# Causal attention between two expert layers on one Trainium2 core: six reads of q on ScalarE's queue, three in each of two steps, become two in each of three steps

## The chip, the cores and the metric

The kernel runs on one core of a Trainium2 chip. The metric is the device time of one execution in microseconds; less is better. The core's engines are TensorE (PE in the profile, its weight loads PEld), VectorE (DVE), ScalarE (ACT), GpSimd (POOL) and SyncE (SP), each with an instruction stream of its own that is worked off in order. They wait for each other on semaphores. SP, ACT and POOL also issue DMA transfers.

## The reference, cut to what matters

A macaron block over 32 sequences of 256 tokens with 128 channels: half an expert layer, causal self-attention, half an expert layer, each with a layer norm ahead and a residual around it. The change lies in the attention.

```python
x = L0_attn_batch                                    # 32 x 256 x 128
x = x + 0.5 * _L0_ffn_ref(_layernorm(x, axis=-1), ...)
x = x + _L0_attn_ref(_layernorm(x, axis=-1), ...)
x = x + 0.5 * _L0_ffn_ref(_layernorm(x, axis=-1), ...)

# inside _L0_attn_ref: 16 heads of 8 channels
qkv = sn_dense(batch, W_qkv, u_qkv, sigma_qkv)
q, k, v = jnp.split(qkv, 3, axis=-1)                 # then split into heads
att = jnp.einsum('bhqd,bhkd->bhqk', q, k) * scale
att = jnp.where(causal[None, None] == 0, big_neg, att)
att = jax.nn.softmax(att, axis=-1)
x = jnp.einsum('bhqk,bhkd->bhqd', att, v)
x = sn_dense(x, W_proj, u_proj, sigma_proj)
```

## The kernel before

The attention works through 32 sequences, one a **turn**. A turn has 12 **steps** (`u` from 0 to 11, `NP = 12`). Each engine has a function `turn(b, k, has)`, written out by hand: it walks through the steps and issues at each what belongs there, for several sequences at once. `has(o)` says whether sequence `b + o` exists. The function `run` emits four turns ahead of the first sequence and the first four, then a hardware loop of seven rounds with four turns each, then the last turns. The order on an engine is thus fixed, and the semaphores alone decide when things start.

What a turn does for the sequences:

- For sequence `b`, each step `u` computes scores by key into the PSUM tile `at_pm` (two buffers, PE L1161 and L1165). ScalarE takes their exponential into `at_pt` (L1080), GpSimd masks that (L1038), and PE multiplies it by `v` some steps later (L1182). PE may write the scores of a step only when ScalarE has taken the exponential of two steps before: `wait(pe, exped, b * NP + (u - 1))`.
- For sequence `b + 2` (and `b + 1`), PE computes scores by query (`at_pp`, L1143 to L1150) from which VectorE takes each query's maximum (L1296). The first of these for a new sequence stands in step 5 and waits for the reads of `q` and `k` (`qk_in`).
- For sequence `b + 3`: transposition of the normalised rows (L1194, copy by ScalarE L1083), projection to `q` and `k` (L1201, L1202), splitting into three bf16 parts (L1091, L1308, L1104, L1049), and the round through DRAM that brings them into the layout of the heads. SyncE writes the parts to `at_qkd` (L1005) and reads `k` back into `kb` with six transfers (L1012). ScalarE reads `q` back into `qs` with six transfers (L1128). These reads wait for the write to have landed (`part_out`).
- For sequence `b + 1`: the negated maxima in bf16 parts are transposed (PE L1242), copied by ScalarE (L1117) into `at_mt`, and at the end of step 8 moved into six rows of `qs` by a transfer of ScalarE's queue (L1119). The first scores by key of the next turn wait for it (`m_in`).
- For sequence `b - 2`: statistics (DVE L1272 to L1276), the power of the variance on GpSimd (L1043), the second normalisation (DVE L1280), its transposition (PE L1198).

The six reads of `q` are two halves (`r` = 0, 1) of 48 rows. Each half is cut into 24, 16 and 8 rows. Before the change ScalarE issues the three reads of half 0 behind the exponential of step 9 and the three of half 1 behind that of step 10. They are issued in program order by the same sequencer that starts the exponentials, so the exponential of step 10 stands behind three issues, and so does that of step 11.

Of the kernel before, what the change touches and what calls it, by code (L numbers as in the profile page):

```python
# [34 lines left out]
NQ = 4  # L35
# [6 lines left out]
def ds(start, n):  # L42
    return bass.ds(start, n)
# [851 lines left out]
def attention(nc, m, io, c, x_dram):  # L895
# [9 lines left out]
    with ctx:  # L905
# [52 lines left out]
        def wait(eng, s, n, most=None):  # L958

            if isinstance(n, int):  # L960
                n = n if most is None else min(n, most)
                if n <= 0:
                    return
            eng.wait_ge(s, n)

        def dma_count(b, slots, each=1):

            return lambda k: b * (16 * each // slots) + (16 * each - (k % slots) * (16 * each // slots))
# [10 lines left out]
        def run(eng, turn):  # L979
            emit = turns(turn)  # L980
            next(emit)
            with eng.Fori(1, B // NQ - 1) as i:
                for k in range(NQ):
                    turn(i * NQ + k, k, lambda o: True)
            next(emit)
# [84 lines left out]
        @blk.scalar  # L1070
        def _(act):
            a = nc.scalar
            act.wait_ge(zeroed, NZ)

            def turn(b, k, has):
                for u in range(NP):
                    if has(0):
                        wait(act, main_done, b * NP + (u + 1))
                        wait(act, pv_done, (b - 1) * PER_CG + (u // 3 + 1))
                        a.activation(pt[u % RING][:, :], pm[u % 2], ACT.Exp, scale=SCALE).then_inc(exped, 1)  # L1080
                    if u == 0 and has(3):
                        wait(act, xt_tr, (b + 4) * TPB)
                        a.activation(xt[(k + 1) % 2][:, :], mi[0][:, 0:S], ACT.Copy).then_inc(xt_out, 1)  # L1083
                    if u == 3 and has(-2):
                        wait(act, x2t_tr, (b - 1) * TPB)
                        a.activation(x2t[k % 2][:, :], mi[1][:, 0:S], ACT.Copy).then_inc(x2t_out, 1)
                    if u == 2 and has(3):
                        h = (k + 1) % 2
                        wait(act, qk_mm, b + 4)
                        wait(act, part_out[h], dma_count(b + 1, 2, 2)(h))  # L1090
                        a.activation(part[h][:, 0:6:5, :], mi[0].rearrange("p (a n) -> p a n", a=2), ACT.Copy).then_inc(a_done, 1)  # L1091
                    if u == 6 and has(-2):
                        wait(act, num_mm, b - 1)
                        a.activation(c.num[:, ds((b - 2) * TPB, TPB), :], mi[0][:, 0:TPB * E].rearrange("p (j e) -> p j e", e=E),
                                     ACT.Copy).then_inc(num_out, 1)
                    if u == 4 and has(-1):
                        wait(act, pv_done, b * PER_CG)
                        wait(act, otr, b - 2)
                        a.activation(ot[(k - 1) % 2][:, :, :].rearrange("p g q -> p (g q)"), po[(k - 1) % 2],
                                     ACT.Copy).then_inc(ot_out, 1)  # L1100
                    if u == 4 and has(3):
                        h = (k + 1) % 2
                        wait(act, r_done, b + 4)
                        a.activation(part[h][:, 1:5:3, :], rest[h][:, :].rearrange("p (a n) -> p a n", a=2), ACT.Copy).then_inc(b_done, 1)  # L1104
                    if u == 5 and has(3):
                        wait(act, v_mm, b + 4)
                        wait(act, pv_done, b * PER_CG)
                        a.activation(vp[(k + 3) % NQ][:, :, :, 0:HD].rearrange("p j h d -> p (j h) d"),
                                     mi[0][:, 0:TPB * D].rearrange("p (h d) -> p h d", d=HD), ACT.Copy).then_inc(v_out, 1)
                    if u == 7 and has(-1):  # L1110
                        wait(act, ont_tr, b)
                        a.activation(ont[(k - 1) % 2][:, :], mi[1][:, 0:S], ACT.Copy).then_inc(ont_out, 1)
                    if u == 8 and has(1):
                        q = (k + 1) % NQ
                        wait(act, mt_tr, b + 2)
                        wait(act, m_in[(q - 2) % NQ], dma_count(b - 1, NQ)(q - 2))
                        a.activation(mt[q % 2][:, :], mi[0].bitcast(BF16)[0:3 * H, 0:S], ACT.Copy).then_inc(mt_out, 1)  # L1117
                        wait(act, mt_out, b + 2)
                        act.dma_start(qs[q][ROWS:ROWS + 6, :, :], mt[q % 2][:, :].unsqueeze(1)).then_inc(m_in[q], 16)  # L1119
                    if u in (9, 10) and has(3):  # L1120
                        n, q, h, r = b + 3, (k + 3) % NQ, (k + 1) % 2, u - 9
                        if r == 0:
                            wait(act, main_done, (n - NQ + 1) * NP)
                            wait(act, part_out[h], dma_count(n, 2, 2)(h))
                        src = qkd[h].rearrange("(a g) n -> a g n", g=HP)
                        for row, size in ((0, 24), (24, 16), (40, 8)):
                            to = 48 * r + row
                            act.dma_start(qs[q][to:to + size, :, :], src[48 * r:48 * r + size, :, :]).then_inc(qk_in[q], 16)  # L1128
            run(act, turn)

        @blk.tensor
# [260 lines left out]
```

## Time and profile before

| | us |
|---|---|
| median of 3 runs | 1376.95 |
| lowest and highest of the 3 | 1375.21, 1379.9 |
| the profiled execution, its own time | 1371.16 |
| the profiled execution's span | 1369.4 |
| PE busy in the span | 1025.8 (75%) |
| ACT busy in the span | 596.7 (44%) |

The span is the time from the first to the last instruction of the program. The profile is of one execution. Its page gives for each engine the busy time, then the span in 40 slices, and further views of the trace answer who waited for whom and list instructions in order of time. A row of the timeline has the start in us from the span's start, the length in us, the engine, the line, the operation, the tiles written and read, the shape, the number of merged instructions and, in brackets, how long the engine had been idle before it and what ended that. ACTq and SPq are the sequencers' issues of transfers; they do not count as busy time of the engine.

### The profile page before, as it was taken

Reading aid. Unit: us, or ns where it says so; the run is one execution under the profiler, and the core shown is the slowest. Engines: PE = TensorE matmul, PEld = TensorE weight load, DVE = VectorE, ACT = ScalarE, POOL = GpSimd, SP = SyncE. Lnnn points to the kernel's source line nnn. Section 1 sums busy time; section 2 is a strip of 40 time slices with the busy share of each in tenths; the row PEclk is TensorE's granted clock in tenths of the full one; section 3 lists DMA queues with packets and bytes.
Section 4 is the critical chain, followed back from the end, with each engine's and each line's share of the span. In section 5 each row is a group of like instructions: output and inputs, shape, how many; then the busy total and the mean of one; then the engine's idle time right before and its main releaser. Section 6 shows DMA issues by size and latency. Waiting matters only on the chain. (4 is left out here: it accounts for less than half of the span.)

```text
span 1369.4 us, 29600 instructions
## 1 busy us (share of the span) xinstructions
PE 1025.8 (75%) x8390; PEld 783.3 (57%) x8390; DVE 735.9 (54%) x2124; ACT 596.7 (44%) x1498; POOL 644.3 (47%) x1022
## 2 busy tenths in 40 slices
PE   1586735787777479999999999999866636777776
PEld 1475515677677246566656566556545515767776
DVE  6476792222222367777777777777626782222212
ACT  4023303334334146666666666666533303434434
POOL 3350005666665135565555555555530006666664
PEclk9657956999989599999999999999977857999989
DMA  4350001111111354445454554444200001111110
GB/s 139 86 159 6 0 0 38 42 43 40 40 40 30 70 102 92 95 96 94 100 99 97 99 99 98 103 99 91 57 17 0 0 0 43 41 43 42 38 42 25
DMA packets 115112, 83.72 MB, mean 61 GB/s; under 512 B 13307, under 2 KB 105523, under 8 KB 115030
## 3 DMA queue, kind: packets, MB, share of 16 engines
q1 hardware_dynamic: 90262, 46.85, 15.8%
q10 hardware_dynamic: 15552, 17.71, 6.1%
q0 software_dynamic: 9216, 18.15, 5.2%
q8 instruction: 42, 0.69, 0.2%
q14 instruction: 40, 0.33, 0.1%
HBM read 52.23 MB, written 30.67 MB: 61 GB/s over the span
## 5 line engine op out<-in xcount | busy, mean ns | idle before, releaser
L1296 DVE TENSOR_REDUCE at_mx<-at_pp 128x2 f32<-128x512 f32 (+1 forms) x384 | 260.4, 686 | 102.6 <-PE at_pp L1150 60.6
L1038 POOL TENSOR_SCALAR_AFFINE_SELECT at_pt<-at_pt 128x256 f32<-128x256 f32 (+1 forms) x384 | 183.3, 488 | 216.6 <-ACT at_pt L1080 215.9
L1080 ACT ACTIVATE at_pt<-at_pm 128x512 f32<-128x512 f32 x384 | 224.4, 597 | 123.4 <-PE at_pm L1161 78.3
L807 ACT ACTIVATE e_ht<-e_ps_h,b1t 128x128 f32<-128x128 f32 x576 | 163.7, 375 | 213.9 <-remote 93.3
L775 POOL DMA_INDIRECT e_x<-rows,gidx x144 | 140.4, 975 | 241.7 <-issue 143.0
L835 PE MATMUL e_ps_h<-e_xnt,e_w1own 128*128 128x128 f32 x1152 | 178.1, 303 | 89.6 <-ACT e_xnt L801 58.8
L835 PEld LDWEIGHTS e_ps_h<-e_xnt,e_w1own 128*128 128x128 f32 x1152 | 162.1, 217 | 98.2 <-ACT e_xnt L801 63.1
L881 DVE SCALAR_TENSOR_TENSOR e_y<-e_ps_y,e_x 128x256 f32<-128x256 f32 x72 | 30.6, 425 | 304.9 <-PE e_ps_y L845 149.1
L845 PE MATMUL e_ps_y<-w,e_ht 128*128 x1152 | 178.3, 299 | 13.2 <-issue 13.0
L845 PEld LDWEIGHTS e_ps_y<-w,e_ht 128*128 128x128 f32 x1152 | 155.9, 208 | 15.9 <-issue 13.1
L1161 PE MATMUL at_pm<-qs,kb 128*128 128x256 bf16 x512 | 98.7, 274 | 20.0 <-ACT at_pt L1080 19.9
L1182 PE MATMUL at_po<-at_pt,vp 128*32 128x256 f32 (+1 forms) x2048 | 111.7, 336 | 1.0 <-POOL at_pt L1038 1.0
L784 POOL DMA_INDIRECT out_dram<-e_y,sidx x72 | 76.6, 1063 | 65.4 <-DVE e_y L881 48.7
L784 POOL DMA_INDIRECT x<-e_y,sidx x72 | 76.3, 1060 | 65.9 <-DVE e_y L881 49.4
L1148 PE MATMUL at_pp<-kb,qs 96*128 96x512 bf16 x256 | 100.2, 392 | 1.7 <-DVE at_mx L1296 0.8
L801 ACT ACTIVATE e_xnt<-e_ps_x 128x256 f32<-128x256 f32 x72 | 28.2, 392 | 139.0 <-PE e_ps_x L828 124.3
L1182 PEld LDWEIGHTS at_po<-at_pt,vp 128*32 128x32 f32 x2048 | 54.0, 110 | 51.0 <-issue 15.4
L1161 PEld LDWEIGHTS at_pm<-qs,kb 128*128 128x128 bf16 x512 | 47.3, 98 | 61.8 <-DMA qs<-at_mt 17.1
L656 DVE SCALAR_TENSOR_TENSOR r_beats<-r_ps_b,r_amax,tie 128x256 f32<-128x256 f32 x128 | 56.9, 482 | 33.6 <-PE r_ps_b L597 33.6
L1150 PE MATMUL at_pp<-mask,identb 128*128 128x256 bf16 x256 | 71.1, 278 | 0.0
L875 DVE COPY e_w1own<-w 128x512 f32 x144 | 61.5, 429 | 16.6 <-remote 12.6
L597 PE MATMUL r_ps_b<-r_batcht 128*128 128x256 f32 x256 | 68.2, 390 | 0.0
(257 smaller groups left out, 1737.2 us busy)
## 6 DMA issues: line engine op xcount, KB each, us to landing
at_qkd<-at_part SPq DMA_DIRECT2D x64, 192.0 KB, 2.9
kb<-at_qkd SPq DMA_DIRECT2D x64, 96.0 KB
qs<-at_qkd ACTq DMA_DIRECT2D x64, 96.0 KB
rows<-ts_x ACTq DMA_DIRECT2D x16, 264.0 KB, 2.9
rows<-at_x SPq DMA_DIRECT2D x32, 132.0 KB, 3.9
ts_x<-in_x_dram SPq DMA_DIRECT2D x16, 256.0 KB, 3.5
at_xa<-x SPq DMA_DIRECT2D x32, 128.0 KB, 3.4
qs<-at_qkd ACTq DMA_DIRECT2D x64, 64.0 KB
```

The source lines that it names most:

```text
L775: pool.indirect_dma_start(x_row[s][:, j % 2, :], None, rows, bass.IndirectOffsetOnAxis(ap=c.gidx[:, j:j + 1], axis=0)).then_inc(x_in[s], 16)
L784: pool.indirect_dma_start(y_dram, bass.IndirectOffsetOnAxis(ap=c.sidx[:, j:j + 1], axis=0), y_row[s][:, j % 2, :], None, bounds_check=T - ...
L807: last = a.activation(hid_t[j % NB][:, f, :], ps_h[j % NB][:, f, :], ACT.Gelu, bias=c.b1t[:, ds(e, 1), f])
L835: last = te.matmul(ps_h[j % NB][:, f, :], w1_own[j % NB][:, f * P:(f + 1) * P], xn_t[(j // 2) % NX][:, j % 2, :], start=True, stop=True, s ...
L845: last = te.matmul(out, hid_t[j % NB][:, f, :], c.w2[:, ds(e, 1), f, :].rearrange("p a d -> p (a d)"), start=False, stop=(f == FC - 1))
L1038: g.affine_select(out=tile, in_=tile, compare_op=ALU.is_ge, fill=0.0, base=0, pattern=[[0, n], [1, P]], channel_multiplier=-1).then_inc(ma ...
L1080: a.activation(pt[u % RING][:, :], pm[u % 2], ACT.Exp, scale=SCALE).then_inc(exped, 1)
L1148: te.matmul(out, qs[s][0:ROWS, v - 4, P:S], kb[s][0:ROWS, v - 4, :, :].rearrange("p r q -> p (r q)"), start=True, stop=False, skip_group_c ...
L1150: te.matmul(out.rearrange("p (r q) -> p r q", r=2)[:, :, P:S], c.identb[:, :], c.mask[:, 0:2, :], start=False, stop=True, skip_group_check ...
L1161: last = te.matmul(out[:, i * S:(i + 1) * S], kb[s][:, g + 2 * w + i, r, 0:P], qs[s][:, g + 2 * w + i, :], start=True, stop=True)
L1182: last = te.matmul(out[32 * j:32 * j + 32, (half + 1) * S - cols:(half + 1) * S], values[:, w // 2, at:at + 32], src[:, i * cols:(i + 1) * ...
L1296: v.tensor_reduce(out, src, axis=AX.X, op=ALU.max).then_inc(maxed, 1)
```

## The change

The condition `u in (9, 10)` becomes `u >= 9`. Steps 9, 10 and 11 each issue one size (24, 16, 8 rows) for both halves. The two waits (`main_done`, `part_out`) stay at the first of the six. Nothing is added or removed: the same six transfers with the same bytes on the same queue and the same semaphore `qk_in`.

```diff
-                    if u in (9, 10) and has(3):
-                        n, q, h, r = b + 3, (k + 3) % NQ, (k + 1) % 2, u - 9
-                        if r == 0:
+                    if u >= 9 and has(3):
+                        n, q, h = b + 3, (k + 3) % NQ, (k + 1) % 2
+                        if u == 9:
                             wait(act, main_done, (n - NQ + 1) * NP)
                             wait(act, part_out[h], dma_count(n, 2, 2)(h))
                         src = qkd[h].rearrange("(a g) n -> a g n", g=HP)
-                        for row, size in ((0, 24), (24, 16), (40, 8)):
+                        row, size = ((0, 24), (24, 16), (40, 8))[u - 9]
+                        for r in range(2):
                             to = 48 * r + row
                             act.dma_start(qs[q][to:to + size, :, :], src[48 * r:48 * r + size, :, :]).then_inc(qk_in[q], 16)
```

In the loop's body, ScalarE's rows from the copy of the maxima in step 8 (L1117) to the second exponential of the next turn stand like this before the change. L1080 are the exponentials, L1119 is the transfer of the maxima, L1128 the reads of `q`, L1083 the copy of the transposed rows.

```order
L1117 ACTIVATE at_mt<-at_mi 48x256
L1119 DMA qs<-at_mt 6x8x256
L1080 ACTIVATE at_pt<-at_pm 128x512
L1128 DMA qs<-at_qkd 24x2048
L1128 DMA qs<-at_qkd 16x2048
L1128 DMA qs<-at_qkd 8x2048
L1080 ACTIVATE at_pt<-at_pm 128x512
L1128 DMA qs<-at_qkd 24x2048
L1128 DMA qs<-at_qkd 16x2048
L1128 DMA qs<-at_qkd 8x2048
L1080 ACTIVATE at_pt<-at_pm 128x512 x2
L1083 ACTIVATE at_xt<-at_mi 128x256
```

The last row but one is the exponential of step 11 and that of the next turn's step 0, with nothing between them. The same place on ScalarE with the change:

```order
L1117 ACTIVATE at_mt<-at_mi 48x256
L1119 DMA qs<-at_mt 6x8x256
L1080 ACTIVATE at_pt<-at_pm 128x512
L1129 DMA qs<-at_qkd 24x2048 x2
L1080 ACTIVATE at_pt<-at_pm 128x512
L1129 DMA qs<-at_qkd 16x2048 x2
L1080 ACTIVATE at_pt<-at_pm 128x512
L1129 DMA qs<-at_qkd 8x2048 x2
L1080 ACTIVATE at_pt<-at_pm 128x512
L1083 ACTIVATE at_xt<-at_mi 128x256
```

The exponential of step 10 now stands behind two issues, that of step 11 behind two more, and two have moved past it to stand ahead of the exponential of step 0. The instructions of the other engines keep their order.

## Rows read from the trace of the kernel before

**Rows 1.** The page: busy time in us and its share of the span.

```profile
PE 1025.8 (75%) x8390; PEld 783.3 (57%) x8390; DVE 735.9 (54%) x2124; ACT 596.7 (44%) x1498; POOL 644.3 (47%) x1022
```

**Rows 2.** Windows of the attention: length, then busy time of PE, PEld, DVE, ACT, POOL, clock, DMA share, GB/s.

```profile
700.00:800.00 100.00, 93.52 (x925) 60.12 (x922) 73.88 (x189) 63.15 (x129) 58.57 (x124) 1.00 0.52 99
```

**Rows 3.** Waits in total: us, times, longest.

```profile
PE at_pm L1161 <- ACT at_pt L1080: 19.9, 32, 2.4
```

**Rows 4.** Timeline of PE from step 11 to step 0 of two turns.

```profile
704.92 0.39 PE L1161 MATMUL at_pm<-qs,kb 128*128 128x256 bf16 x2 [0.61 <-ACT at_pt L1080]
...
720.34 0.27 PE L1150 MATMUL at_pp<-mask,identb 128*128 128x256 bf16 x1
721.24 0.38 PE L1161 MATMUL at_pm<-qs,kb 128*128 128x256 bf16 x2 [0.63 <-ACT at_pt L1080]
```

**Rows 5.** Timeline of ScalarE, from the transfer of step 8 to step 1 of the next turn.

```profile
717.97 0.75 ACTq L1119 DMA_DIRECT2D qs<-at_mt  x1
718.91 0.60 ACT L1080 ACTIVATE at_pt<-at_pm 128x512 f32<-128x512 f32 x1 [0.97 <-PE at_po L1182]
719.01 1.31 ACTq L1128 DMA_DIRECT2D qs<-at_qkd  x3
720.49 0.60 ACT L1080 ACTIVATE at_pt<-at_pm 128x512 f32<-128x512 f32 x1 [0.98 <-PE at_pm L1165]
720.51 1.30 ACTq L1128 DMA_DIRECT2D qs<-at_qkd  x3
721.98 1.08 ACT L1080 ACTIVATE at_pt<-at_pm 128x512 f32<-128x512 f32 x2 [0.89 <-PE at_pm L1161]
722.95 0.39 ACT L1083 ACTIVATE at_xt<-at_mi 128x256 f32<-128x256 f32 x1
723.35 1.15 ACT L1080 ACTIVATE at_pt<-at_pm 128x512 f32<-128x512 f32 x2
```

**Rows 6.** All issues of L1128: duration in ns, min/median/max.

```profile
L1128 ACTq DMA_DIRECT2D qs<-at_qkd x192: 295/374/1017, 463.6 to 967.3; - x192
```

**Rows 7.** Timeline: the three issues behind step 9, each alone.

```profile
719.01 0.31 ACTq L1128 DMA_DIRECT2D qs<-at_qkd  x1
719.35 0.37 ACTq L1128 DMA_DIRECT2D qs<-at_qkd  x1
719.75 0.58 ACTq L1128 DMA_DIRECT2D qs<-at_qkd  x1
```

**Rows 8.** Timeline from step 1 to step 4: GpSimd, VectorE, PE.

```profile
724.49 1.01 POOL L1043 TENSOR_TENSOR at_x<-at_vare,at_powers 128x4 f32<-128x4 f32 x1
725.53 0.60 DVE L1280 TENSOR_SCALAR at_xn<-at_x 128x128 f32<-128x128 f32 x2 [1.10 <-POOL at_x L1043]
726.19 0.44 PE L1198 MATMUL at_mi<-ident,at_xn 128*128 128x128 f32 x2
727.39 0.71 PE L1214 MATMUL at_mi<-wv,at_xt 128*128 128x128 f32 x4 [0.21 <-DVE at_rest L1308]
```

**Rows 9.** Timeline of the first turn: the transfer of the maxima, and the weight load that waits for it.

```profile
487.23 0.89 ACTq L1119 DMA_DIRECT2D qs<-at_mt  x1
489.84 0.11 PEld L1161 LDWEIGHTS at_pm<-qs,kb 128*128 128x128 bf16 x2 [0.55 <-DMA qs<-at_mt]
```

**Rows 10.** SyncE's reads of k and their first use on PE, in a middle turn and in a late one.

```profile
718.88 4.37 SPq L1012 DMA_DIRECT2D kb<-at_qkd  x6
727.93 0.38 PE L1143 MATMUL at_pp<-kb,qs 96*128 96x256 bf16 x2
964.98 4.34 SPq L1012 DMA_DIRECT2D kb<-at_qkd  x6
973.58 0.39 PE L1143 MATMUL at_pp<-kb,qs 96*128 96x256 bf16 x2 [0.33 <-DMA kb<-at_qkd]
```

**Rows 11.** Windows around those reads, columns as in Rows 2.

```profile
721.00:727.00 6.00, 5.70 (x60) 3.62 (x60) 4.30 (x14) 4.13 (x9) 4.08 (x8) 1.00 0.93 170
727.00:731.00 4.00, 3.79 (x42) 2.72 (x41) 3.32 (x8) 3.10 (x7) 1.85 (x3) 1.00 0.01 2
```

## The prediction

> **What bounds the kernel now.** I read the page first, to see where TensorE is full. PE is the busiest engine, 1025.8 us [rows 1]. The windows then show how full PE is within the attention: 93.52 us busy in 100, at granted clock 1.00, VectorE 73.88, ScalarE 63.15 [rows 2]. So a turn of the attention has only 7% of idle time on PE, and a change can give back no more than what part of that it reaches. The length of a turn is read from PE's first scores of step 0 in two turns: 721.24 - 704.92 = 16.32 us [rows 4], of which 7% is 1.1 us.
>
> The list of waits names the largest piece: the scores by key of L1161 wait for ScalarE's exponentials 32 times, 19.9 us together, 0.62 us a turn [rows 3]. The timeline says which scores these are. They are those of step 0: PE ends L1150 at 720.34 + 0.27 = 720.61 and starts them at 721.24, idle 0.63 us, released by L1080, and the turn before the same with 0.61 us [rows 4]. They need the exponential of step 10, the one at 720.49, which ends at 721.09 [rows 5].
>
> Why is that exponential late? ScalarE sat idle 0.98 us before it. The bracket names PE's L1165, but what stands directly ahead of it in the program are three issues of reads, from 719.01 for 1.31 us, to 720.32. The exponential starts 0.17 us later. The same again: three issues from 720.51 for 1.30 us, to 721.81, and the exponential of step 11 at 721.98, 0.17 us later [rows 5]. Had PE set the time, the distance of 0.17 would not come out the same twice. In these steps ScalarE's sequencer, not its arithmetic and not its input, sets the pace.
>
> **The change, step by step.** All times are those of this turn [rows 5 to 7].
>
> *Step 9.* The issues cost 0.31, 0.37 and 0.58 us with gaps of 0.04 us. Two of them end at 719.72 instead of 720.32. The exponential of step 10 then starts at 719.72 + 0.17 = 719.89 and ends at 720.49, 0.60 us earlier. PE has its own work until 720.61. So the scores of step 0 can start at about 720.65, 0.59 earlier, if nothing else holds them.
>
> *Step 10.* The next two issues follow at 719.91. The third issue of a batch took 0.58 us where the median of all 192 is 0.374; I take 0.58 for the first of the two (it is the third in a row, and comes just where that one came) and 0.37 for the other, with 0.04 between: to 720.90. The exponential of step 11 starts at 721.07 instead of 721.98.
>
> *Step 11, where the two moved issues cost something.* From 721.09 two at 0.41, a little over the median, and 0.04 between them: to 721.95, and the exponential of step 0 at 722.12. Before, it stood right behind that of step 11: the two together end at 721.98 + 1.08 = 723.06, so it started at about 722.46. It comes 0.34 us earlier, not 0.59. Behind it are the copy L1083 (722.95 before, 722.61 now; its input from L1194 would be there 0.59 earlier) and the exponential of step 1 (723.35 before). They too come 0.34 us earlier, 0.41 if the last two issues take the median.
>
> *What is late next.* From the exponential of step 1 a chain leads to PE: the mask, the power at 724.49 behind it on GpSimd, the normalisation L1280 that waited 1.10 us for it, and the transposition L1198 at 726.19, right when L1280 ends at 726.13; L1214 waits 0.21 us on VectorE behind that [rows 8]. These come earlier by what the exponential of step 1 gains. So PE wins 0.59 us at step 0 and gives about 0.2 back at steps 2 to 4. What is left for the turn is the gain of ScalarE's row of issues, 0.34 to 0.41 us; I take 0.38.
>
> *What the change costs at nothing.* The bytes are the same. The DMA engines are 0.93 busy from 721 to 727 and idle from 727 on [rows 11]. SyncE's reads of k are issued from 718.88 to 723.25, ScalarE's last now until 721.95 instead of 721.81 [rows 5, 10]; so the last transfers to land are still those of SyncE's queue. Their first use is at 727.93 [rows 10], 0.9 us after the traffic stops. That is the cover of the moved reads; with a turn that reaches step 5 some 0.4 us earlier it shrinks to about 0.5.
>
> A rule of the Trainium skill speaks against any gain here. "DMA: Bandwidth & Descriptors", section "Issuing engines are not separate DMA queues", says that the time a sequencer needs to start a transfer is usually small beside the transfer. By it the position of six issues would be worth next to nothing, and the time would stay at 1377. The trace does not bear it out for this place, since 1.31 us of issue stand ahead of an exponential that PE waits for. The same section says that transfers of all queues share 16 DMA engines and interleave; with that the trace agrees, and by it the later reads neither gain nor lose.
>
> *The sum.* The exponentials run in 32 turns. Reads of q stand beside them in 29, those that have a sequence b + 3. I leave the first of these out, which fills the pipeline: 28 turns by 0.38 us = 10.6 us. The profiled execution took 1371.16 us, so it would take 1360.5. It lies 5.8 us below the median of the three runs shown, 1376.95, and I add that back: **1366.3 us**, 0.8% faster.
>
> **Bounds.** The unknown price is what an issue takes in its new place. The lowest of the 192 is 0.295, the third of a batch 0.58, the longest 1.017 us [rows 6, 7]. With 0.37 for all of the last four, PE's own floor of 0.59 us a turn is reached: 16.5 us, 1360.4. With the mean of the batches instead (1.30 us for three, 0.43 each with its gap), the row gains what was reckoned, 0.3 to 0.4 us. The break-even is worked out like this. From the exponential of step 10 at 719.89 to 722.46, where that of step 0 stood, are 2.57 us. Two starts (0.02 and 0.17 us each) and two gaps take 0.46, so four issues may take 2.11, 0.53 each.
>
> **The rivals.**
>
> *The whole wait goes (chance 0.08).* The last four issues take the median or less and the copy L1083 is held by PE alone. For it: the median. Against it: three issues in a row take 1.31 and 1.30, not 1.2. Gain 0.55 to 0.62 a turn, 1360.
>
> *A landing holds PE in place of the exponential (0.13).* There are two places. One is the transfer of the maxima, for which the same scores of step 0 wait. In the first turn, where no exponential hides it, PE's weight load came 489.84 - 487.23 = 2.61 us after its issue [rows 9]. In the turn above that is 717.97 + 2.61 = 720.58, just ahead of PE's own 720.61; it costs nothing, but 0.4 us more would eat most of the gain. The other is the first use of k and q in step 5. In a late turn PE waited for it, 973.58 - 964.98 = 8.60 us after SyncE's first read [rows 10]. In the turn above that is 718.88 + 8.60 = 727.48, where the forecast wants PE at 727.93 - 0.38 = 727.55. So the gain ends at 0.45 a turn, and if the reads land 0.4 later in most turns, it is gone: 1373 to 1377.
>
> *Slower (0.08).* The moved issues are as slow as the third of a batch, 0.58 each, because ScalarE and SyncE issue at once. Then: 719.91 + 1.20 = 721.11, exponential of step 11 at 721.28, two more until 722.50, exponential of step 0 at 722.67, 0.21 us later than before. The copy, the exponential of step 1 and the chain to L1198 follow: 28 by 0.21 = 5.9 us, 1383. It decides from 0.53 us an issue on. For it: SyncE issues until 723.25. Against it: the second batch took 1.30 for three while SyncE was issuing too.
>
> The likeliest case has 0.71, its own range is 1361 to 1371 (0.2 to 0.55 us a turn).
>
> **How the numbers follow.** A difference under 0.3%, 4.1 us, is about what a measurement of this kernel can't tell from none. The first rival and most of the likeliest case are faster by more: 0.08 + 0.70 = 0.78. The landing case and the rest are the same: 0.14. Slower 0.08. The range from 1359 to 1375 takes in both good cases and the better part of the landing case; above it lie the rest of that and the slower one.
>
> **What the profile of the changed kernel would show.** Pairs of issues instead of triples, 0.7 to 0.8 us behind step 9; the exponential of step 10 some 1.0 us behind that of step 9 instead of 1.58; PE's wait ahead of step 0 near zero, total far below 19.9; the exponential of step 0 no longer right behind that of step 11; a turn of 15.9 us instead of 16.3; a new wait of PE at L1198 of about 0.2 us. The prediction is wrong if pairs take over 1.1 us in steps 10 and 11, if PE's wait only changes its name to a transfer (the maxima at step 0, or kb and qs at L1143), or if the time goes while PE's wait stays.

## The result: 0.27% faster, a third of the forecast

The changed kernel takes 1374.68 us (median of 22 runs), the kernel before 1376.85 us (median of 22). The ratio is 0.9973, interval 0.9961 to 0.9985: 2.1 to 5.4 us are gained, 3.7 in the middle. (The two medians lie 2.2 us apart and the two means 3.6; gains in time are given by the ratio, here and below.) The forecast was 10.6 us.

The profiled execution of the changed kernel has a span of 1375.3 us at a mean granted clock of 0.865. Its page has these busy times.

```profile
PE 1039.5 (76%) x8359; PEld 790.3 (57%) x8390; DVE 737.2 (54%) x2124; ACT 595.6 (43%) x1498; POOL 646.4 (47%) x1022
```

In the view of waits, two lines answer to [rows 3] (engine, its line, what it waited for: us in total, times, the longest). Line numbers from the edit on are one higher than before.

```profile
PE at_pm L1162 <- ACT at_pt L1080: 4.1, 5, 2.1
PE at_mi L1199 <- DVE at_xn L1281: 16.8, 31, 3.4
```

Of the 32 waits of [rows 3], 19.9 us together, 5 with 4.1 us are left. The wait at the transposition L1199 is 16.8 us. In the kernel before that list had this line for it:

```profile
PE at_mi L1198 <- DVE at_xn L1280: 12.2, 15, 3.4
```

It comes twice as often after the change. By the timelines PE waits 0.21 us there in an ordinary turn, where it waited for nothing before, and 0.68 instead of 0.52 us in a turn at the loop's end. So the change did what it says, and a part came back where the forecast expected it.

ScalarE's timeline of one turn, to be read against [rows 5] (start in us, duration, what; q behind the engine's name means its queue issues a transfer; in brackets the idle time before and who ended it):

```profile
723.23 0.75 ACTq L1119 DMA_DIRECT2D qs<-at_mt  x1
724.17 0.60 ACT L1080 ACTIVATE at_pt<-at_pm 128x512 f32<-128x512 f32 x1 [0.97 <-PE at_pm L1162]
724.27 0.72 ACTq L1129 DMA_DIRECT2D qs<-at_qkd  x2
725.15 0.60 ACT L1080 ACTIVATE at_pt<-at_pm 128x512 f32<-128x512 f32 x1 [0.39 <-PE at_pm L1162]
725.17 1.17 ACTq L1129 DMA_DIRECT2D qs<-at_qkd  x2
726.50 0.60 ACT L1080 ACTIVATE at_pt<-at_pm 128x512 f32<-128x512 f32 x1 [0.75 <-PE at_pm L1162]
726.52 0.78 ACTq L1129 DMA_DIRECT2D qs<-at_qkd  x2
727.48 0.60 ACT L1080 ACTIVATE at_pt<-at_pm 128x512 f32<-128x512 f32 x1 [0.38 <-PE at_po L1183]
727.98 0.38 ACT L1083 ACTIVATE at_xt<-at_mi 128x256 f32<-128x256 f32 x1
728.24 1.09 ACT L1080 ACTIVATE at_pt<-at_pm 128x512 f32<-128x512 f32 x2
```

Three pairs, 0.72, 1.17 and 0.78 us. The exponential of step 10 stands 0.98 us behind that of step 9 (725.15 - 724.17). The pair behind it is the dear one. The single issues of the second and third pair:

```profile
725.17 0.54 ACTq L1129 DMA_DIRECT2D qs<-at_qkd  x1
725.74 0.60 ACTq L1129 DMA_DIRECT2D qs<-at_qkd  x1
726.52 0.43 ACTq L1129 DMA_DIRECT2D qs<-at_qkd  x1
726.98 0.32 ACTq L1129 DMA_DIRECT2D qs<-at_qkd  x1
```

PE, at the place of [rows 4]:

```profile
725.60 0.27 PE L1151 MATMUL at_pp<-mask,identb 128*128 128x256 bf16 x1
725.89 0.38 PE L1162 MATMUL at_pm<-qs,kb 128*128 128x256 bf16 x2
```

The scores of step 0 start 0.02 us behind the matmul ahead of them (725.60 + 0.27 = 725.87), where it was 0.63 us.

### The end of the loop

The attention's loop body holds four turns, k = 0 to 3. The fourth (k = 3) ends with the loop's branch, right behind step 11. The loop has six rounds, not seven as the section on the kernel before says: it is `Fori(1, B // NQ - 1)` with B = 32 and NQ = 4 and works through sequences 4 to 27; the first four sequences are written out ahead of it and the last four behind it. So it jumps back five times, and "the turn at the loop's end" is one of those five. I had read no such turn. Here is one in the kernel before:

```profile
750.64 0.75 ACTq L1119 DMA_DIRECT2D qs<-at_mt  x1
...
753.20 1.22 ACTq L1128 DMA_DIRECT2D qs<-at_qkd  x3
754.58 1.12 ACT L1080 ACTIVATE at_pt<-at_pm 128x512 f32<-128x512 f32 x2 [0.80 <-PE at_pm L1161]
```

and in the changed kernel:

```profile
755.16 0.75 ACTq L1119 DMA_DIRECT2D qs<-at_mt  x1
...
758.38 0.60 ACT L1080 ACTIVATE at_pt<-at_pm 128x512 f32<-128x512 f32 x1 [0.70 <-PE at_pm L1162]
758.39 0.86 ACTq L1129 DMA_DIRECT2D qs<-at_qkd  x2
759.78 0.60 ACT L1080 ACTIVATE at_pt<-at_pm 128x512 f32<-128x512 f32 x1 [0.81 <-PE at_po L1183]
...
771.93 0.74 ACTq L1119 DMA_DIRECT2D qs<-at_mt  x1
```

Before, the exponentials of steps 11 and 0 form one row of two. After, the last pair of issues ends at 758.39 + 0.86 = 759.25, and the exponential of step 0 starts 0.53 us behind it, where it was 0.18 in the ordinary turn (727.48 - 726.52 - 0.78). From the issue L1119 it stands 759.78 - 755.16 = 4.62 us off. PE feels it twice (in an ordinary turn it has no such wait at L1166, and 0.21 us at L1199):

```profile
760.43 0.40 PE L1166 MATMUL at_pm<-qs,kb 128*128 128x128 bf16 x4 [0.28 <-ACT at_pt L1080]
...
763.85 0.44 PE L1199 MATMUL at_mi<-ident,at_xn 128*128 128x128 f32 x2 [0.68 <-DVE at_xn L1281]
```

The last round ends with the same instructions, but there the loop doesn't jump back. In the changed kernel:

```profile
953.08 0.85 ACTq L1129 DMA_DIRECT2D qs<-at_qkd  x2
954.17 0.60 ACT L1080 ACTIVATE at_pt<-at_pm 128x512 f32<-128x512 f32 x1 [0.50 <-PE at_po L1183]
```

Here the exponential of step 0 starts 954.17 - 953.08 - 0.85 = 0.24 us behind the last issue, where it is 0.53 to 0.55 in all five turns with the jump.

### All turns together

The table is worked out from the timelines: a turn runs from one issue L1119 to the next, and each entry is a median over the turns of that kind in one trace: 15 ordinary ones, from the loop's second round on, and the five at the loop's end. "Stretch" is from the third of these issues to the last, 29 turns, and leaves the start-up out. The names are those of the experiments below.

| kernel | ordinary turn | turn at the loop's end | stretch | six issues of q, in order |
|---|---|---|---|---|
| before | 16.33 | 16.71 | 474.1 | .31 .37 .62 .39 .38 .41 |
| before, again (e6) | 16.32 | 16.71 | 473.3 | |
| changed | 16.01 | 16.77 | 468.7 | .31 .38 .53 .60 .50 .32 |
| changed, again (e5) | 16.02 | 16.77 | 468.7 | |
| sizes in the new order, three and three (e8) | 16.46 | 16.95 | 478.0 | .31 .38 .68 .45 .65 .32 |
| pairs, sizes in the old order (e1) | 15.84 | 16.53 | 465.4 | .31 .37 .47 .54 .32 .33 |
| the same, again (e11) | 15.70 | 16.52 | 465.7 | |
| last pair in the next turn (e4) | 15.71 | 16.08 | 459.0 | .30 .38 .53 .60, .28 .36 |
| the same, again (e12) | 15.71 | 16.09 | 459.1 | |
| changed, SyncE quiet meanwhile (e7) | 16.19 | 16.20 | 470.5 | .31 .38 .32 .44 .28 .32 |
| before, SyncE quiet meanwhile (e10) | 16.78 | 16.79 | 490.1 | .31 .37 .33 .30 .38 .33 |
| last two of the old order in the next turn (e9) | 16.29 | 16.47 | 475.2 | .30 .37 .46 .54, .32 .33 |
| changed, old order in the start-up (e2) | 16.00 | 16.76 | 469.1 | |
| changed, old order where k is 3 (e3) | 16.00 | 16.71 | 467.5 | |

The stretches can be read from one row each. These are the rows of the tile at_mt in the window from the third turn on (count, shortest, median and longest issue in ns, first and last start), of the kernel before, of the changed one, and of both again (e6, e5):

```profile
L1119 ACTq DMA_DIRECT2D qs<-at_mt x30: 741/748/782, 520.6 to 994.7; - x30
```

```profile
L1119 ACTq DMA_DIRECT2D qs<-at_mt x30: 740/748/781, 527.4 to 996.1; - x30
```

```profile
L1119 ACTq DMA_DIRECT2D qs<-at_mt x30: 740/748/782, 522.5 to 995.8; - x30
```

```profile
L1119 ACTq DMA_DIRECT2D qs<-at_mt x30: 741/748/782, 521.5 to 990.2; - x30
```

474.1 and 473.3 us before, 468.7 and 468.7 after: 5.0 us gained in the mean, 1.3 more than the middle of the timing and within its interval. So the gain is made where the forecast put it, and all but a little of what can be told apart lies there.

The start-up, the first two turns, shows where a single trace misleads. In the changed kernel they took 527.4 - 492.4 = 35.0 us, against 520.6 - 487.2 = 33.4 before. At that place TensorE's granted clock was 0.57 in this execution (columns as in [rows 2]):

```profile
498.00:502.00 4.00, 3.45 (x14) 2.38 (x15) 0.35 (x1) 2.45 (x6) 1.46 (x3) 0.57 0.87 118
```

I first took the 1.6 us for a cost of the new order. The experiments e2, e3 and e5 are against it.

### The profile page after: what moved, and what is told of

Same layout as the page of the kernel before. It is cut to its first block and busy times, and to the rows that moved or that the text cites. A ratio compares the mean times of both kernels' runs of the same rounds, so it can differ in the third digit from the quotient of the medians.

```text
span 1375.3 us, 29569 instructions
## 1 busy us (share of the span) xinstructions
PE 1039.5 (76%) x8359; PEld 790.3 (57%) x8390; DVE 737.2 (54%) x2124; ACT 595.6 (43%) x1498; POOL 646.4 (47%) x1022
## 5 line engine op out<-in xcount | busy, mean ns | idle before, releaser
L1080 ACT ACTIVATE at_pt<-at_pm 128x512 f32<-128x512 f32 x384 | 226.1, 599 | 116.7 <-PE at_pm L1162 75.1
L845 PE MATMUL e_ps_y<-w,e_ht 128*128 x1152 | 187.6, 304 | 33.0 <-issue 32.9
L881 DVE SCALAR_TENSOR_TENSOR e_y<-e_ps_y,e_x 128x256 f32<-128x256 f32 x72 | 30.6, 425 | 311.5 <-PE e_ps_y L845 187.0
L845 PEld LDWEIGHTS e_ps_y<-w,e_ht 128*128 128x128 f32 x1152 | 161.1, 211 | 42.6 <-issue 39.9
L1183 PEld LDWEIGHTS at_po<-at_pt,vp 128*32 128x32 f32 x2048 | 53.8, 110 | 50.8 <-issue 14.6
```

Of the source, the lines that this page charges most:

```text
L845: last = te.matmul(out, hid_t[j % NB][:, f, :], c.w2[:, ds(e, 1), f, :].rearrange("p a d -> p (a d)"), start=False, stop=(f == FC - 1))
L1183: last = te.matmul(out[32 * j:32 * j + 32, (half + 1) * S - cols:(half + 1) * S], values[:, w // 2, at:at + 32], src[:, i * cols:(i + 1) * ...
```

## The experiments

The kernels e1 to e4 ran on a chip on which every kernel was about 7% shorter (the kernel before took 1279.16 us there, its experts' stages were the shorter part), so their ratios and their turns are compared, not their times. In the diffs, `plan` lists for steps 9, 10 and 11 what is read: (half of the heads, first row, rows). Each is given against the changed kernel, but for e10.

### e1: pairs, in the order of sizes that the kernel had before

The diff is two edits: it spreads the issues over three steps, and it reads equal sizes of both halves together (24, 24, 16, 16, 8, 8 in place of 24, 16, 8, 24, 16, 8). This kernel makes the first alone.

```
-                        row, size = ((0, 24), (24, 16), (40, 8))[u - 9]
-                        for r in range(2):
+                        plan = (((0, 0, 24), (0, 24, 16)), ((0, 40, 8), (1, 0, 24)), ((1, 24, 16), (1, 40, 8)))
+                        for r, row, size in plan[u - 9]:
```

> Two issues a step as in the changed kernel, but in the order of sizes of the kernel before (24, 16 then 8, 24 then 16, 8). Theory 'place' (an issue is slow because of where it stands behind the first two, whatever its size): the pairs of steps 10 and 11 take as long as in the changed kernel, about 1.15 and 0.85 us, the exponential of step 0 starts 4.3 us after the transfer of step 8, the turn is 16.0 us. Rival 'size' (the two reads of 16 rows side by side are dear): the pair of step 10 falls to 0.8 to 0.9 us, the turn to 15.8 us, and the time to 3 us below the changed kernel. In both, the start-up turn is as short as before the change (14.7 us, no half clock), since the order in it is that of before: 2 us below the changed kernel from that alone.

Measured: 1267.79 against 1279.16 us, ratio 0.9898 (0.9871 to 0.9925). The placement alone is worth more than the whole diff. Its stretch is 943.2 - 477.8 = 465.4 us, its pairs are cheaper than those of the changed kernel (.47 and .54 in step 10, .32 and .33 in step 11). On the chip of e11 the same code gained less, 0.6%.

### e2: the order of before in the start-up

```
+                        plan = NEW if has(0) else OLD
```

NEW and OLD stand for the orders of the changed kernel and of the one before.

> The changed kernel, but the turns ahead of the first exponentials keep the order 24, 16, 8, 24, 16, 8. Theory 'start-up': the order alone makes the six issues 0.57 us longer in the last of these turns, TensorE idles 2.03 instead of 1.46 us and its clock is halved for some 4 us; with the old order the first turn is 14.7 instead of 16.6 us, and the time is 2 us below the changed kernel, about 4 us below the kernel before (ratio 0.997 to 0.996). Rival 'chance': the half clock was an accident of that profile; then the ratio stays at 0.9973 and the first turn shows no fixed relation to the order.

Measured: 1272.85 us, ratio 0.9946 (0.9928 to 0.9964). Its first two turns took 473.4 - 441.5 = 31.9 us:

```profile
L1119 ACTq DMA_DIRECT2D qs<-at_mt x3: 741/762/889, 441.5 to 473.4; - x3
```

That looked as if the start-up were the culprit, until the next run.

### e3: the order of before in the turns at the loop's end

```
+                        plan = OLD if k == 3 and has(0) else NEW
```

> The changed kernel, but every fourth turn (the last of a loop round) has three issues in two steps as before. Theory 'loop end': with issues in step 11 the branch of ScalarE stands behind them instead of under the exponential, and the gain of the other turns (0.33 us) is lost in this one; with the old arrangement that turn takes 16.7 us, as in both kernels, and the ratio stays within 0.001 of the changed kernel's. Rival: the loop end costs the same in both; then the last turn of a round loses its 0.33 us, seven times, and the time rises by 2.3 us over the changed kernel's.

Measured: 1274.0 us, ratio 0.9962 (0.9941 to 0.9984). The turn at the loop's end went from 16.77 to 718.17 - 701.45 = 16.72 us:

```profile
701.45 0.75 ACTq L1119 DMA_DIRECT2D qs<-at_mt  x1
...
718.17 0.74 ACTq L1119 DMA_DIRECT2D qs<-at_mt  x1
```

That is the length it has in the kernel before, 16.71. So the new order loses some 0.05 us in each of the five turns with the jump. The edit also reaches the turn ahead of the loop and the one that ends its last round, where nothing jumps back. These get longer with the old order, 16.57 instead of 16.44 and 16.62 instead of 16.25 us. And this kernel starts up in the new order, in 474.6 - 443.5 = 31.1 us, where e2 took 31.9 in the old one:

```profile
L1119 ACTq DMA_DIRECT2D qs<-at_mt x3: 741/762/892, 443.5 to 474.6; - x3
```

The theory of a dear start-up falls with it.

### e4: the last pair in the next turn

ScalarE reads the two pieces of 8 rows in step 2 of the next turn, behind that step's exponential, so nothing is issued in step 11 and nothing stands ahead of the loop's branch. The start-up keeps the order of before.

```
+                    if u == 2 and has(-1) and has(2):
+                        q, h = (k + 2) % NQ, k % 2
+                        src = qkd[h].rearrange("(a g) n -> a g n", g=HP)
+                        for r in range(2):
+                            to = 48 * r + 40
+                            act.dma_start(qs[q][to:to + 8, :, :], src[48 * r:48 * r + 8, :, :]).then_inc(qk_in[q], 16)
```

> Two issues in steps 9 and 10, none in step 11; the two reads of 8 rows are issued in step 2 of the next turn, behind its exponential, where ScalarE waits 0.4 us for PE. The turns ahead keep the old order. Theory 'ScalarE's row of issues is the bound': the exponential of step 0 stands right behind that of step 11, the copy L1083 is set by PE, the turn falls by another 0.2 to 0.3 us to about 15.75, also at the loop's end (16.7 to 16.2): 28 turns by 0.6 = 16 us below the kernel before, ratio 0.989. Rival 'another bound lies close behind' (the landing of q and k at step 5, the power on GpSimd): PE waits at L1144 or L1199 grow by as much, and the ratio stays above 0.994.

Measured: 1261.32 us, ratio 0.9859 (0.9831 to 0.9887). Both kinds of turn are 0.6 us shorter than before, 15.71 and 16.08. The stretch is 931.1 - 472.1 = 459.0 us:

```profile
L1125 ACTq DMA_DIRECT2D qs<-at_mt x30: 741/748/787, 472.1 to 931.1; - x30
```

### e5 and e6: both kernels again

The same code on another chip.

> The changed kernel itself, timed beside the kernel before on the chip of this set. From the turns of its profile (21 turns of 16.33 become 16.01 us, 7 turns at the end of a loop round go from 16.71 to 16.77) the sum is 21 x 0.32 - 7 x 0.06 = 6.3 us. Theory 'the turns are all': the ratio is about 0.995. Rival 'the start-up takes 1.9 us back each time': the first turn of the attention is again 16.6 us and the ratio is 0.997.

> The kernel before once more, for its profile: turns of 16.3 us and 16.7 at the end of a loop round, reads of q at 0.31, 0.37, 0.6, 0.39, 0.38, 0.41 us. Of interest are the first two turns of the attention (14.7 and 18.7 us in the first profile): theory 'chance' has them scatter by 1 us and more between executions of one kernel, with half-clock stretches of TensorE at other places; the theory of an order that costs has them at 33.4 us together again.

Measured: e5 1366.6 against 1370.07 us, ratio 0.9965 (0.9944 to 0.9985); e6, one run, 1369.42. The first two turns took 32.4 us in the changed kernel (489.1 to 521.5) and 32.0 in the one before (490.5 to 522.5).

Over all traces they take 30.6 to 36.0 us, in no relation to the order of the reads: e1 and e11 are the same kernel and stand at the two ends. The median of the ordinary turns repeats within 0.01 us between the two traces of before, of the changed kernel and of e4. In e1 and e11 it differs by 0.14, but there single turns lie between 15.6 and 16.4 us, and the means of the two agree, 15.88 and 15.86.

### e7: SyncE doesn't issue while ScalarE does

In the changed kernel SyncE now begins its reads of k only when the exponential of step 11 is done.

```
+                    if has(0):
+                        sp.sem_inc(passed, 1)
+                        wait(sp, exped, b * NP + NP)
```

> The changed kernel, but SyncE issues its six reads of k only after the exponential of step 11, so ScalarE's six issues run alone. The whole gets slower, since k arrives later (PE waits at step 5); of interest is the price of ScalarE's issues. Theory 'contention with SyncE': the third to the fifth fall from 0.5 to 0.6 us to 0.3 to 0.4 us, the exponential of step 11 starts 2.8 us after the transfer of step 8 instead of 3.27. Theory 'ScalarE's own queue': they stay at 0.5 and 0.6.

Measured (one run): 1366.0 us. ScalarE's pairs, at its own line numbers:

```profile
719.79 0.72 ACTq L1132 DMA_DIRECT2D qs<-at_qkd  x2
...
720.69 0.79 ACTq L1132 DMA_DIRECT2D qs<-at_qkd  x2
...
721.66 0.62 ACTq L1132 DMA_DIRECT2D qs<-at_qkd  x2
```

0.79 and 0.62 us where the changed kernel has 1.17 and 0.78. Everything else on ScalarE's queue is the same, so the surplus comes with SyncE's six reads. For reads of 8 rows at least, e12 says that it is their issuing and not their transfers: its two late reads are issued when SyncE has done issuing its reads of k but the DMA engines are still 0.95 busy, and they take .28 and .36 us, the price that 8 rows have alone. SyncE pays nothing for the company. Its six issues take 4.37 us in the kernel before [rows 10] and here, where ScalarE is silent:

```profile
722.26 4.37 SPq L1015 DMA_DIRECT2D kb<-at_qkd  x6
```

The second 16-row read takes 0.44 us even here, against 0.32 for the first. The time doesn't fall with it, since k now lands too late for step 5:

```profile
PE at_pp L1147 <- DMA kb<-at_qkd: 10.5, 22, 1.0
```

### e8: the order of sizes alone

Three and three, as before, in the order 24, 24, 16 and 16, 8, 8.

```
+                        plan = (((0, 0, 24), (1, 0, 24), (0, 24, 16)), ((1, 24, 16), (0, 40, 8), (1, 40, 8)), ())
```

> Three issues in two steps as before the change, but in the order of sizes of the changed kernel (24, 24, 16, then 16, 8, 8). Theory 'place': the third is slow (0.6 us) whatever it is, the others 0.37 to 0.41, turn 16.3 us, ratio 1.000. Rival 'two of 16 rows in a row are dear': the fourth takes 0.6 too, the exponential of step 11 comes 0.2 us later, the turn is 16.4 to 16.5 us, ratio 1.002 to 1.003.

Measured: 1375.36 against 1370.07 us, ratio 1.0032 (1.0012 to 1.0051). It is slower than the kernel before. Its batches:

```profile
719.40 1.44 ACTq L1129 DMA_DIRECT2D qs<-at_qkd  x3
...
721.02 1.50 ACTq L1129 DMA_DIRECT2D qs<-at_qkd  x3
```

1.44 and 1.50 us for the same six reads that took 1.31 and 1.30 [rows 5]. With e1 and e11 this takes the diff apart: the placement gains 8 us or more, and the order of sizes loses 4 to 5 (4.4 here).

### e9: the last two reads of the old order in the next turn

Built from e1 and e4: 24, 16 in step 9, 8, 24 in step 10, and the second half's 16 and 8 in step 2 of the next turn.

```
+                        for row, size in ((24, 16), (40, 8)):
+                            to = 48 + row
+                            act.dma_start(qs[q][to:to + size, :, :], src[48:48 + size, :, :]).then_inc(qk_in[q], 16)
```

> As the version with a late pair (two reads in steps 9 and 10, two in step 2 of the next turn), but with the sizes in the order of the kernel before: 24, 16, then 8, 24, and late 16, 8. Theory 'PE is the bound there, ScalarE's issues no longer are': cheaper issues change nothing, turn 15.7 us, ratio as with the late pair, 0.986 to 0.988 on whatever chip. Rival 'the row of issues is still the bound': the turn falls by the 0.1 us that the exponential of step 11 gains, to 15.6, 3 us more.

Measured: 1369.52 against 1372.36 us, ratio 0.9992 (0.9971 to 1.0014). No gain, where e4 gains over 1%. The list of waits says why:

```profile
PE at_pp L1150 <- DMA qs<-at_qkd: 10.7, 18, 1.2
```

The same line in e4's second run (e12):

```profile
PE at_pp L1150 <- DMA qs<-at_qkd: 2.5, 5, 1.3
```

In the median the last piece of q lands 9.82 us behind L1119 in e9, against 9.00 in e12, and PE waits for it 18 times. (The expectation named neither outcome: both its theories had the time at or below e4's.) A piece of 16 rows that late is too late, where one of 8 is just in time.

### e10: the kernel before, with SyncE quiet

e7's wait, put into the kernel before.

> The kernel before the change, but SyncE issues its six reads of k only after the exponential of step 11. Theory 'contention with SyncE': the third read of each batch falls from 0.6 to about 0.35 us, each batch of three from 1.3 to about 1.05, the exponential of step 10 starts 2.3 instead of 2.56 us after the transfer of step 8, that of step 11 at 3.5 instead of 4.0. Theory 'a third issue in a row is slow by itself': 0.6 stays.

Measured (one run): 1385.46 us. The batches of three:

```profile
728.08 1.07 ACTq L1131 DMA_DIRECT2D qs<-at_qkd  x3
...
729.33 1.06 ACTq L1131 DMA_DIRECT2D qs<-at_qkd  x3
```

1.07 and 1.06 against 1.31 and 1.30 [rows 5]: in the kernel before, too, each batch paid 0.24 us for SyncE's company. The late k costs more than that gives:

```profile
PE at_pp L1146 <- DMA kb<-at_qkd: 17.6, 28, 1.3
```

### e11 and e12: the two that gained, on one chip

The code of e1 and of e4 again, side by side.

> The kernel with pairs in the order of sizes of before, once more, beside the late pair and beside the kernel before on one chip. The theory that the change is two edits, a placement that gains and an order of sizes that loses, asks for the same turns as in its first run (15.84 us, 16.53 at a loop's end): 21 x 0.49 + 7 x 0.18 = 11.5 us below the kernel before, ratio 0.991 to 0.992. If the ratio is 0.995 or more, as that of the changed kernel, the order is not what took the gain.

> The kernel with the 8-row reads moved to step 2 of the next turn, once more, beside the others. With its turns of 15.71 and 16.08 us: 28 x 0.62 = 17.4 us below the kernel before, ratio 0.987. Rival: the landing of q and k holds PE at step 5, as it does for 0.3 us a turn when the late pair carries 16 and 8 rows; then 0.990 or more, with waits of PE at L1150.

Measured against 1377.67 us: e11 1368.93, ratio 0.9938 (0.9919 to 0.9957); e12 1363.93, ratio 0.9897 (0.9870 to 0.9924). Their stretches:

```profile
L1119 ACTq DMA_DIRECT2D qs<-at_mt x30: 740/748/782, 522.6 to 988.3; - x30
```

```profile
L1125 ACTq DMA_DIRECT2D qs<-at_mt x30: 740/748/787, 527.0 to 986.1; - x30
```

465.7 and 459.1 us. Against the mean of the kernel before, 473.7, that is 8.0 and 14.6 us less, and the ratios say 8.5 and 14.2. For the other two kernels the stretch agrees as well: changed -5.0 (ratios: -3.7 and -4.8), order alone +4.3 (ratio: +4.4). The attention's stretch thus accounts for the timings to within 1.5 us on these chips. Both kernels stay some 3 us below what was expected, 11.5 and 17.4 us, which were again a median turn's gain times a count of turns. On the chip of e1 to e4 the ratios say more than the stretches, 13.0 us for e1 and 18.0 for e4 against 8.3 and 14.7; the kernel before has no trace from that chip, so where the other 3 to 5 us come from stays open. In e12 ScalarE's row from step 10 to step 0 is free of issues at its end:

```profile
720.65 1.17 ACTq L1135 DMA_DIRECT2D qs<-at_qkd  x2
721.99 1.09 ACT L1080 ACTIVATE at_pt<-at_pm 128x512 f32<-128x512 f32 x2 [0.76 <-PE at_pm L1168]
```

The dear pair is still there, 1.17 us, but the exponentials of steps 11 and 0 stand together again. The pair of 8-row reads takes 0.68 us in its new place, where a gap is:

```profile
724.06 0.68 ACTq L1092 DMA_DIRECT2D qs<-at_qkd  x2
```

e12 is the best version: 1% less than the kernel before, and four times the gain of the change.

## Why the prediction was too high

The mechanism, the place and the sign were right; the gain was 3.7 us where 10.6 were forecast. Two terms of the sum were wrong: the gain of a turn, "I take 0.38", and above all the count of turns that have it, "28 turns". That 1374.7 us still lies in the range of 1359 to 1375 is luck. Its upper part was there for a late landing, which didn't happen.

**Step 9, right.** The exponential of step 10 was to come 0.60 us earlier. By the medians it starts 1.92 us behind L1119 instead of 2.56, 0.64 earlier. PE's wait at step 0 was to go to near zero: 19.9 us [rows 3] became 4.1.

**Step 10, mis-sized.** The second pair was put at 0.99 us (0.58 + 0.04 + 0.37) and took 1.17 (0.54 and 0.60). I took the price of an issue by its rank in a batch. The trace of before holds no second 16-row read behind a first one while SyncE issues. e1 has the old neighbours and pays .47 and .54 for this pair, 0.12 us less than the changed kernel, so the new order of sizes accounts for most of the 0.18 us by which the pair was underrated. What lies above the quiet price of .32 and .44 goes with SyncE's issuing (e7).

**Step 11, right in sum.** The third pair was put at 0.86 and took 0.78 in the turn shown (0.82 by the medians of its issues). With the surplus of step 10 the exponential of step 0 comes 0.17 us earlier, 4.32 instead of 4.49, and not 0.34.

**What is late next, right in kind.** The turn depended on the exponential of step 1 and the chain to the transposition; I had moved that exponential by the same amount as the one of step 0. It gained more, 5.08 instead of 5.41, 0.33 us, since with its input ready it starts close behind the copy: 728.24, which is 0.26 us after the copy's start, where it was 0.40 [rows 5]. This gave back what the dear pair took. The ordinary turn is 0.32 us shorter in the median, 16.01 instead of 16.33, close to the 0.38 that I took. The median hides a pattern, though: the first turn of a round gains 0.15 us, the second and the third 0.35. The wait at L1198, now L1199, grew by 4.6 us in all and is 0.21 us in an ordinary turn; 0.2 was forecast.

**The count of turns, the step that failed.** I multiplied one turn's gain by 28, as if all 28 turns were the one that I had read. The timelines, with the mean of two traces of each kernel, say what the 28 did:

| turns | forecast | measured |
|---|---|---|
| five at which the loop jumps back | 1.9 | -0.25 |
| the loop's first turn | 0.4 | -0.8 |
| the other 22 | 8.4 | 6.0 |
| together | 10.6 | 4.9 |

Of the 5.7 us that are missing, 3.3 lie in the six turns that were counted as ordinary and lose, and 2.4 in the size of the gain, 0.27 us in the mean of the others instead of 0.38. (The sum of 6.3 us that went on record with e5 counted seven turns with a loss. Two of them have no jump back, and they gain 0.13 and 0.29 us.)

**The turn at the loop's end** loses 0.06 us in the median (16.77 against 16.71; e3 gives 0.05 back by undoing the change there). What follows the last issue starts 0.53 us behind it in the five turns with the jump back, and 0.24 us behind it at the end of the last round, with the same issues and no jump. The second trace (e5) says the same, 0.53 or 0.54 against 0.23. So some 0.3 us go with the jump. (The loop's first turn has 0.52 too, without a jump; more on it below.) Before the change, ScalarE's sequencer could reach the branch while the exponential of step 11 was running; after it, the sequencer is busy with issues until that exponential is over. That this is why the jump cost less before is argued from the place. It fits that the turn's end takes 0.76 us over an ordinary turn in the changed kernel, which issues in step 11, and 0.37 in e4 and 0.38 before, which don't. What in the jump takes the time, no run tells.

**The loop's first turn** takes 17.23 and 17.45 us in the changed kernel's two traces, 16.80 and 16.27 in those of before. It is the one turn that runs the loop's code for the first time. In 13 of the 14 traces one of ScalarE's six issues is long in it, between 0.83 and 1.70 us, and not always the same one; the second trace of before (e6) has none. In the changed kernel's first trace it took 1.46 us, the longest in the row of all 192:

```profile
L1129 ACTq DMA_DIRECT2D qs<-at_qkd x192: 275/381/1463, 468.5 to 969.3; - x192
```

The turn is as slow in e1, e11 and e8 (17.2 to 17.3 us), and takes 15.95 and 16.06 in e4 and e12. Why an issue is long there, no run tells. Between the 5.0 us of the stretches and the 3.7 of the timing lies less than the interval.

**The rivals.** That the whole wait goes fell with the price of the second pair. The slower case asked for four issues above 0.53 us on average; they took .53, .60, .50 and .32, 0.49, so it was nearer than its 0.08 said. It is what e8 is, with its third and fifth issue at 0.68 and 0.65. The landing case fell for this change: in the median the last piece of q and k lands 8.7 us behind L1119 and PE first uses them at about 9.6, against 9.1 and 9.9 before, so the cover of 0.8 to 0.9 us is still there. Its mechanism is real: it takes e9's gain, and in e7 PE waits 10.5 us for k.

**The rule that I weighed.** The Trainium skill ("DMA: Bandwidth & Descriptors", section "Issuing engines are not separate DMA queues") says that the time to start a transfer is usually small beside the transfer. The runs don't contradict that; what they refute for this place is what I drew from it, that the position of six issues is worth next to nothing. The same bytes, issued in other places and another order, went from 14 us less (e12) to 4 us more (e8). The rule's other half, that a second issuing engine saves only sequencer time, says nothing of what such an engine costs the first one; e7 and e10 show it.

## What to carry to other kernels

Transfers issued on an engine's own queue ahead of an instruction that another engine waits for cost their whole issue time, here 0.3 to 0.6 us each; look for the gap behind the last awaited instruction (e4) before you split the row evenly. A diff that moves issues also gives them new neighbours, and their order of sizes and what another queue issues meanwhile can cost as much as the move brings. Before you multiply a turn's gain by the number of turns, read the turn at the loop's end and the first one too, and count the jumps in the code.

## What the runs showed of the hardware

The price of an issue on ScalarE's queue depends on whether SyncE issues too. Reads of 24, 16 and 8 rows cost ScalarE .31, .37 and .33 us while SyncE is quiet (e10), and up to 0.68 in the median while SyncE issues (e8, third in its batch). It is one-sided: SyncE's six reads of k take 4.37 us with ScalarE's issues beside them (before) and without (e7). Transfers in flight don't raise the price of a read of 8 rows by themselves (e12: .28 and .36 us at a DMA share of 0.95). The order of sizes matters as well: the same six reads take 2.61 us in the order of before and 2.94 in e8. Two 16-row reads in a row are the dearest pair in every kernel that has it as one (1.17 us; 0.79 with SyncE quiet). Why the second costs 0.44 us even alone is open.

A jump back of the loop right behind issues costs ScalarE some 0.3 us: 0.53 us from the last issue to the next exponential with it, 0.24 without. And where the loop's code runs for the first time, one issue takes 0.83 to 1.70 us in 13 of 14 traces.

The median of the attention's ordinary turns repeats within 0.01 us from one execution to the next in three kernels of four, while the first two turns scatter by 5 us for the same code on two chips (e1 36.0, e11 30.6). In the one start-up that I looked at window by window, four microseconds ran at a granted clock of 0.57, near the lower of TensorE's two levels (1.2 of 2.4 GHz). A single trace of such a stretch decides nothing, and it made me chase a cause that wasn't there.
